# Attention over a paged cache: a head's scores are followed by the weighing of the head three back, then by the transposes of the head two back

## What is computed

```python
q, k, v = x @ Wq.T, x @ Wk.T, x @ Wv.T        # 32 query heads, 8 key heads, D = 128
q, k = rope(rmsnorm(q)), rope(rmsnorm(k))
k_all = concatenate([k_cache[block_table], k])  # 512 + 32 keys
v_all = concatenate([v_cache[block_table], v])
scores = einsum('bqhd,bkhd->bhqk', q, k_all) * SCALE
probs = softmax(where(valid, scores, -1e30))
o = einsum('bhqk,bkhd->bqhd', probs, v_all)
x = x + o @ Wo.T
```

## Time and profile before

| | us |
|---|---|
| median of 3 runs (lowest to highest) | 2366.05 (2365.11 to 2367.28) |
| the profiled execution | 2365.88 |
| its span, first to last instruction | 2364.0 |
| PE busy | 2277.7 (96%) |
| DVE busy | 1789.2 (76%) |
| ACT busy | 1307.5 (55%) |
| POOL busy | 1146.2 (48%) |
| attention stage on PE | about 763 to 1990 |

### The profile page before, as it was taken

One profiled execution on the slowest core, in us unless ns is written; L12 is line 12 of the kernel. 1 busy time (PEld: TensorE's weight loads), 2 busy tenths in 40 slices (PEclk: granted clock), 3 DMA queues, 4 the chain that ended last, 5 costly groups with the idle time before them and its releaser, 6 DMA issues. The chain is left out here.

```text
span 2364.0 us, 52334 instructions
## 1 busy us (share of the span) xinstructions
PE 2277.7 (96%) x16384; PEld 1963.0 (83%) x16384; DVE 1789.2 (76%) x3551; ACT 1307.5 (55%) x2667; POOL 1146.2 (48%) x1218
## 2 busy tenths in 40 slices
PE   6998999999995999999999999999999997999999
PEld 6877777777773899999999999999999996888887
DVE  8851899999995888888888888888888886422222
ACT  6723888888874555555555555555555554311111
POOL 4200444444443677777777777777777773000000
PEclk9999999999997999999999999999999998999999
DMA  7533233233325788888888888888888885643442
GB/s 264 204 108 103 67 112 110 93 110 111 110 80 168 261 294 294 280 281 290 293 287 290 289 298 290 290 280 282 293 292 291 288 295 178 210 139 95 128 136 62
DMA packets 447144, 493.27 MB, mean 209 GB/s; under 512 B 95317, under 2 KB 390229, under 8 KB 438742
## 3 DMA queue, kind: packets, MB, share of 16 engines
q1 hardware_dynamic: 410198, 357.98, 47.4%
q0 software_dynamic: 36864, 134.23, 16.3%
HBM read 399.83 MB, written 92.27 MB: 208 GB/s over the span
## 5 line engine op out<-in xcount | busy, mean ns | idle before, releaser
L1096 POOL TENSOR_TENSOR att_probs<-att_probs,att_inverse 128x512 f32<-128x512 f32 x512 | 535.3, 1045 | 287.2 <-DVE att_inverse L1292 282.8
L1200 ACT ACTIVATE att_probs<-att_probs,att_low 128x544 f32<-128x544 f32 x512 | 383.9, 750 | 515.3 <-DVE att_low L1279 448.6
L1157 PE MATMUL att_o<-att_probs_t,att_values 128*128 128x128 f32 x4096 | 540.9, 275 | 0.0
L1279 DVE CUSTOM_DVE_ANT_0 att_probs<-att_score,att_mask,att_batch_cols 128x544 f32<-128x544 f32 x512 | 399.9, 781 | 137.4 <-PE att_score L1122 99.4
L1157 PEld LDWEIGHTS att_o<-att_probs_t,att_values 128*128 128x128 f32 x4096 | 497.6, 192 | 0.0
L1288 DVE COPY att_probs_t<-att_turn 128x512 f32<-128x512 f32 x512 | 350.9, 685 | 1.2 <-PE att_turn L1137 1.2
L1082 POOL DMA_INDIRECT att_values<-L_cond_v_cache,att_v_rows_of x256 | 283.5, 1107 | 82.6 <-POOL att_v_rows_of L1078 50.1
L1122 PE MATMUL att_score<-att_keys_raw,att_queries_raw 128*128 128x288 f32 (+1 forms) x1024 | 290.4, 407 | 26.8 <-DMA att_queries_raw<-q_t 24.6
L1137 PE MATMUL att_turn<-ident,att_probs 128*128 128x128 f32 x2048 | 311.1, 274 | 1.2 <-POOL att_probs L1096 0.8
L791 PE MATMUL proj_proj<-x3t_hi,proj_w_hi 128*128 128x512 f32 x640 | 267.2, 417 | 6.7 <-DVE proj_w_lo L851 6.7
L1255 DVE TENSOR_TENSOR att_keys_lo<-att_keys_raw,att_keys_hi 128x384 fp32r<-128x384 f32 (+1 forms) x320 | 260.5, 815 | 16.2 <-ACT att_keys_hi L1193 16.2
(11 more groups left out here) (132 smaller groups left out, 3958.2 us busy)
## 6 DMA issues: line engine op xcount, KB each, us to landing
att_keys_raw<-L_cond_k_cache SPq DMA_DIRECT2D x1024, 128.0 KB
q_t<-proj_q_out SPq DMA_DIRECT2D x32, 1024.0 KB, 3.9
att_queries_raw<-q_t SPq DMA_DIRECT2D x64, 512.0 KB
o_t<-att_heads_out SPq DMA_DIRECT2D x64, 512.0 KB, 6.7
out_o_raw<-o_t SPq DMA_DIRECT2D x32, 1024.0 KB, 5.7
maps_even<-L_cond_weight SPq DMA_DIRECT2D x8, 1024.0 KB, 12.4
maps_odd<-L_cond_weight SPq DMA_DIRECT2D x8, 1024.0 KB, 16.3
w_nat<-L_cond_Wq SPq DMA_DIRECT2D x8, 1024.0 KB, 5.6
```

Source lines behind the costliest of these rows:

```text
L1096: nc.gpsimd.tensor_tensor(probs[:, k, 0:L], probs[:, k, 0:L], inverse[:, k:k + 1].to_broadcast([P, L]), ALU.mult).then_inc(probs_ready, 1)
L1157: last = nc.tensor.matmul(o, values[j][:, t, h * D:(h + 1) * D], probs_t[m % 2][:, t * P:(t + 1) * P], start=(t == 0), stop=False, skip_gr ...
L1200: nc.scalar.activation(probs[:, k, :], probs[:, k, :], ACT.Exp, bias=low[k][:, 0:1], scale=-1.0, accum_out=total[k][:, 0:1]).then_inc(exp_ ...
L1279: nc.vector.tensor_tensor_reduce(out=probs[:, k, :], in0=score_ps[:, LEFT:LEFT + KEYS], in1=mask[j][:], scale=batch_cols[j][:, h:h + 1], s ...
```

## The change

In each step of PE the calls of `weigh` and `turn` change places. The same instructions, with the same waits, are issued; the calls behind the loop, which finish the last heads, stay as they are.

```diff
             def pair(i, first):
                 for n in range(N):
                     scores(i, n)
+                    if n >= 3 or not first:
+                        weigh(i, n - 3)
                     if n >= 2 or not first:
                         turn(i, n - 2)
-                    if n >= 3 or not first:
-                        weigh(i, n - 3)
 
             pair(0, True)
             with pe.Fori(1, PAIRS) as i:
```

## The result

The changed kernel takes 2471.5 us (median of 4 runs, 2467.1 to 2472.6) against 2365.6 (4 runs) before: ratio 1.0443, 95% interval 1.0425 to 1.0461. It is 106 us slower. The forecast was 2477, range 2440 to 2525. The profiled execution took 2472.6 us, its span is 2470.8.

The account below looks back on a forecast made before the run. PE bounds the attention stage, 18.86 of 19.05 us a batch. A pass becomes 2 x 20.44 + 0.43 + 2 x 0.1, rounded to 41.6 against 38.1; 31.8 passes add 111 to 2366: 2477 us, range 2440 to 2525.

Parts of the forecast that it names:

- term 2: The ring in the attention stage: turn, DVE's copy, weighing, next turn, with one head in it, takes 2.40 us.
- term 3: Heads with new values: their four products stand between weighing and turn, so the ring takes 3.02 us.
- term 4: DVE's masking path fits the ring by 0.07 us, except 0.43 us once a pass at its edge; slow splits add 0.
- term 1: The turn starts 0.90 us later in PE's step, which removes at most 0.19 us of waits a batch, 12 us.
- (b): A gain: the copy's round trip hides behind the scores, only waits on POOL's probabilities go: 2354 us; chance 3%.
- (c): Hardly any change: the ring binds but for a few hundredths, paid by the freed waits: 2362 to 2370 us; chance 4%.
- term 5: The first weighing of a group of four waits for ACT's copy-out of the group before: 0.1 us a batch.
- (a): Heavier DVE: every split runs at 1.0 us beside POOL, 2510 to 2535 us; chance 9%.
- (d): The clock: PE is granted less once it idles in every head; over 3500 us at half clock; chance 3%.

Follow-up runs that it names:

- e4: The changed kernel with DVE's splits of the next keys and queries cut to a few columns: 2468.9 us, ratio 1.0437 to the kernel before.
- e2: The changed kernel with ACT copying four heads out before its piece of the split: 2469.4 us, ratio 1.0440 to the kernel before.
- e10: The changed kernel with the register for DVE's wait on the old weighing computed ahead of both waits: 2457.4 us, ratio 1.0389 to the kernel before.
- e1: The changed kernel with DVE's copy waiting for the old weighing before it waits for the transposes: 2480.6 us, ratio 1.0489 to the kernel before.
- e3: The changed kernel with DVE doing its piece of the split before the copy instead of behind it: 2511.6 us, ratio 1.0614 to the kernel before.
- e5b: The changed kernel with DVE's copy taking only 128 of 512 columns: 2423.6 us, ratio 1.0252 to the kernel before.
- e7b: The changed kernel's order, weigh before turn, only in steps 0 to 3, the old order elsewhere: 2448.3 us, ratio 1.0360 to the kernel before.
- e12: The changed kernel with weighing four heads back instead of three, early copy-out, and DVE's split before its copy: 2431.3 us, ratio 1.0278 to the kernel before.
- e9: The changed kernel with DVE's copy cut to 128 of 512 columns and ACT copying out before its split: 2398.1 us, ratio 1.0143 to the kernel before.

## Why the prediction was right

**The ring (term 2), 2.40 us: right, 2.38.** Its parts were less so: turn to copy 0.64 (0.66 forecast), copy to weighing 0.74 to 0.75 (0.84), weighing to turn 0.99 to 1.00 (0.90). In the earlier trace rows the 0.84 ran up to the first matmul of a turn in the bare handshake; here the weighing starts 0.09 sooner and then takes 0.09 to 0.10 longer. That this is the same tenth, paid in another place, is argued and not shown; two parts of the sum were off by 0.09 in opposite directions, and the sum held.

**Heads with new values (term 3), 3.02: 2.90 to 2.91,** which is 1.38 to 1.46 up to the weighing and 1.44 to 1.53 from there. The 0.10 added for what follows the products shows elsewhere: the turn behind them has a record of 0.66 instead of 0.60, and its copy starts later. In the native one of the two steps (h = 2) the transpose of the new group does not hide behind the copy, as the prediction had it: the weighing follows PE's own work at 1.46, and loses no time in restarting. Timelines of PE, DVE and ACT of the changed kernel:

```profile
1508.12 0.66 PE L1137 MATMUL att_turn<-ident,att_probs 128*128 128x128 f32 x4
...
1509.75 1.16 PE L1157 MATMUL att_o<-att_probs_t,att_values 128*128 128x128 f32 x8 [0.21 <-ACT att_heads_out L1222]
```

```profile
1508.90 0.69 DVE L1288 COPY att_probs_t<-att_turn 128x512 f32<-128x512 f32 x1 [0.97 <-PE att_turn L1137]
```

```profile
1509.12 0.57 ACT L1222 ACTIVATE att_heads_out<-att_o 128x512 f32<-128x512 f32 x1
```

**The DVE path (term 4): half right.** That it fits into the ring was right (e4). That the slow splits leave POOL's shadow was right as well: 384 columns took 604 ns in the mean (909 before), and one of three is still grazed (0.70 against 0.55). But the 0.43 us for the edge of a pass did not come. In both batches of a pass the mask of the first head starts right behind the reciprocal:

```profile
1512.46 0.15 DVE L1292 RECIPROCAL att_inverse<-att_total 128x1 f32<-128x1 f32 x1
1512.54 0.78 DVE L1279 CUSTOM_DVE_ANT_0 att_probs<-att_score,att_mask,att_batch_cols 128x544 f32<-128x544 f32 x1
...
1533.20 0.15 DVE L1292 RECIPROCAL att_inverse<-att_total 128x1 f32<-128x1 f32 x1
1533.27 0.77 DVE L1279 CUSTOM_DVE_ANT_0 att_probs<-att_score,att_mask,att_batch_cols 128x544 f32<-128x544 f32 x1
```

The 0.60 of the earlier trace rows was taken for a fixed cost of the branch, against 0.10 elsewhere. That was misread: the row itself puts 0.45 of it down to PE's scores, and in the kernel before the same distance is 0.35 where there is no edge:

```profile
1509.66 0.15 DVE L1292 RECIPROCAL att_inverse<-att_total 128x1 f32<-128x1 f32 x1
1510.01 0.78 DVE L1279 CUSTOM_DVE_ANT_0 att_probs<-att_score,att_mask,att_batch_cols 128x544 f32<-128x544 f32 x1 [0.20 <-PE att_score L1122]
```

So the edge's own share was 0.25 at most. It did cost something before: the mask at 1529.21 comes 1.49 us behind the start of its scores, the one at 1510.01 only 1.23, and that step of PE takes 2.44 instead of 2.25. In the changed kernel the first masks of both batches come 1.35 to 1.36 behind their scores (which start at 1511.18 and 1531.92), so the edge costs nothing there. That DVE's sequencer now gets through the branch while the engine works is only argued.

**The waits that the turn loses (term 1), at most 0.19 us a batch:** they were not waits for POOL. The group of the turns in the kernel before, 900 to 1900 us, has 0.8 us of them:

```profile
L1137 PE MATMUL att_turn<-ident,att_probs 128*128 128x128 f32 x1680 | 254.8, 274 | 0.8 <-POOL att_probs L1096 0.8
```

Half of the 0.19 is the edge just told (0.19 in one of two batches). So the 12 us on which rivals (b) and (c) counted were not to be had from a later turn.

**The copy-out (term 5), 0.1 us a batch: 0.04,** by e2, in one of the two weighings that wait for it.

**What the forecast did not have:** the later copies. Even heads pay 0.08 to 0.12 us for a register instruction between two waits (e10), and behind new values the copy comes 0.06 later still and the weighing 0.84 instead of 0.75 behind it. That weighing is the first of its group. In the compiled program its wait for the copy is an instruction of its own in front, as the weighing itself waits for the copy-out. It is the pattern that cost 0.07 on DVE in e1, though no run takes it away on PE. The steps 1, 3, 5 and 7 take 2.50 + 2.59 + 2.47 + 2.62 us, which is 0.66 a batch more than four plain rings of 2.38, 1.3 in a pass; the copy-out's 0.04 is in it.

**The sum.** Forecast 41.6 us for a pass, measured 41.45 (16 x 1000 / 386). What did not come is the edge (0.43), the longer products with new values (4 x 0.11), 0.02 of each of 12 plain rings (0.24), the copy-out's 0.2 and the rounding up (0.09): 1.4 us. What came instead are the 1.3 us of late copies. The pass is right to 0.4% (and its increase, 3.5 forecast and 3.35 measured, to 4%) because errors of opposite sign met, and that is luck. The decision, slower by some 100 us, rests on the ring alone.

**The rivals.** (a), the heavier DVE, did not come in this kernel, but its mechanism is real: e3, e5b, e7b and e12 are cases of it. (b), a gain, needed a round trip under 1.35; it was 1.38 to 1.63 from turn to weighing, so for native heads it missed by 0.03 us and not by the 0.15 that the forecast gave it, and e9 shows seven of eight steps at PE's pace once the copy is short. (c), hardly any change, needed a ring within a few hundredths of PE's own pace, and split heads alone lose 0.28 each. (d), the clock: 1.00 over the stage (763 to 2095 us), though PE idles in every head; only in its first microseconds (769 to 772) is it 0.50, as it is before.

## What to carry to other kernels

In a pipeline written out by hand, what matters is how much of the producer's own work stands between an operation and the one that needs its result through another engine. Here the same instructions with scores alone in between (0.85 to 0.92 us) can't hide a round trip of 0.95 behind the transposes (1.38 less 0.43; the forecast had 1.07), and with the scores and a weighing they can. Where the scores nearly cover it, the restart of the waiting instruction costs more than the wait. Look for such round trips bare, at the end or the start of a stage, where nothing hides them: the sum read there held to 0.02 us, though its parts did not. And a bound engine can look busy at 98% while it does 8% less: count its instructions. When a ring is opened, look at once for the next chain, and at which engines' operations come to lie side by side (e3, e12).

## What the runs showed of the hardware

- Where a VectorE split with two SBUF inputs and a GpSimd product overlap, one waits for the other, but the records' starts don't say which. The splits that start at 1508.53 (e3) and 1518.72 (e5b), ahead of multiplies at 1508.65 and 1518.94, end 0.43 us behind those, at 1510.13 and 1520.42, as did the split of the earlier trace rows, which started second. In e3 it also goes the other way. The product for new_group that starts 0.10 us behind a split takes 0.85 us, and 726 ns in the mean of 900 to 1900 us against 403 in the changed kernel:

```profile
1517.27 0.69 DVE L1255 TENSOR_TENSOR att_keys_lo<-att_keys_raw,att_keys_hi 128x512 fp32r<-128x512 f32 x1
...
1517.37 0.85 POOL L1101 TENSOR_TENSOR att_new_group<-att_probs,att_inverse 128x128 f32<-128x128 f32 x1
```

  The Trainium skill (SBUF — State Buffer, "SBUF: two separate sides") says that whichever starts first gets the pair and the other blocks. The last case agrees with it; the splits of e3 and e5b do not, by the starts of their records. When they started, GpSimd's gather before the multiply was still running by its record (from 1507.66 for 0.98 us in e3); a gather alone does not hold a split up (one beside it takes 0.55 us at 1509.51 in the changed kernel). GpSimd's spans are rough in a profile, so by which time an operation counts as started is open.
- What stands in front of a waiting instruction counts when the handshake is exposed. If the copy itself waits for the transposes, it starts 0.64 us behind them; if a wait of its own in front does, 0.70 to 0.71 (e1); if a register instruction in front does, 0.72 to 0.76 (the changed kernel; e10 takes the instruction away and has 0.64).
- A weighing that has to wait before it may load its operands takes 0.99 to 1.00 us up to the next operation instead of 0.89 to 0.90.
